# A six-layer attention stack on one core: scores, mask and maxima by halves of the heads, with a transposition between the halves

## The reference

```
def local_attention(q, k, v):          # w = 32, nw = 16 windows of a sequence
    bq = q.reshape(b, h, nw, w, d)
    bk = k.reshape(b, h, nw, w, d)
    ...                                # keys: the window before and the own one, 64 in all
    # sim = 8 * (q . k), masked to the 33 last keys, softmax over the 64 keys, times v
for each of 6 layers, each sequence:
    q, k, v = shift_tokens(x) @ Wqkv;  q, k = l2norm(.) * scale, rotary
    x = x + local_attention(q, k, v) @ Wo
    x = x + feed-forward(layernorm(shift_tokens(x)))
```

## Time and profile before

| what | value |
|---|---|
| median of 3 runs | 1909.38 us (1898.79, 1909.38, 1910.66) |
| the profiled execution's own time | 1898.89 us |
| its span, first to last instruction | 1897.1 us |
| PE busy | 1606.4 us, 85% |
| DVE busy | 1250.9 us, 66% |
| ACT busy | 989.3 us, 52% |
| the stack, first to last scores | 572.0 to 1414.8 us |
| granted TensorE clock | mean 0.927; 0.99 from 700 to 1200 us |

### The profile page before, as it was taken

How to read it: one execution, slowest core, us unless ns; L and a number is a source line. 1 busy time by engine, 2 the same in 40 slices (tenths; PEclk the granted TensorE clock), 3 DMA queues, 4 the chain that set the end, 5 groups by cost and what they waited for, 6 DMA issues and landing times.

```text
span 1897.1 us, 42488 instructions
## 1 busy us (share of the span) xinstructions
PE 1606.4 (85%) x17121; PEld 1091.3 (58%) x17121; DVE 1250.9 (66%) x2351; ACT 989.3 (52%) x1861; POOL 762.1 (40%) x1082
## 2 busy tenths in 40 slices
PE   3005476999878999999999999999987999999999
PEld 1002264676645666656666666666664677677676
DVE  6846694212957878878878778888864666666211
ACT  1034133333335667756767566666654776677332
POOL 0000030100357676776776667766740333334000
PEclk6556797899978999999999999999999999999999
DMA  3000002010032323322323232332230000000111
GB/s 111 19 6 0 3 1 63 22 35 15 1 108 52 92 74 81 84 71 70 93 73 80 76 77 64 92 83 60 57 87 1 1 1 1 1 1 1 34 34 34
DMA packets 74572, 88.23 MB, mean 47 GB/s; under 512 B 22994, under 2 KB 42936, under 8 KB 74346
## 3 DMA queue, kind: packets, MB, share of 16 engines
q1 hardware_dynamic: 73562, 85.28, 17.3%
q10 hardware_dynamic: 816, 0.24, 0.1%
HBM read 35.21 MB, written 2.34 MB: 20 GB/s over the span
## 4 chain that ended last, share of the span: by engine, by line
PE 60%; DVE 27%; issue 6%; ACT 4%; DVEq 1%; DMA 1%; POOL 0%; ACTq 0%; POOLq 0%; SPq 0%
PE PS L1412 8%; PE PS L1132 6%; PE PS L1123 6%; PE PS L1664 4%; PE PS L2162 4%; DVE st_t L1456 3%; PE PS L2119 3%; PE PS L1542 3%; PE PS L2141 3%; DVE st_r L1448 3%; DVE st_ss L1461 3%; DVE st_den L1581 2%; PE PS L1779 2%; PE PS L1616 2%; PE PS L1521 2%
## 5 line engine op out<-in xcount | busy, mean ns | idle before, releaser
L1490 POOL TENSOR_TENSOR st_r<-st_r,st_t 128x512 f32<-128x512 f32 x192 | 243.8, 1276 | 193.0 <-DVE st_t L1456 193.0
L1412 PE MATMUL PS<-st_wqkv,st_xs 128*128 128x512 f32 x576 | 306.1, 616 | 14.3 <-DVE st_t L1456 8.8
L2266 POOL TENSOR_SCALAR la_p<-la_p,la_rden 128x589 f32<-128x589 f32 x64 | 112.9, 1764 | 229.8 <-DVE la_rden L2285 229.8
L1448 DVE TENSOR_TENSOR st_r<-PS,st_rot 128x512 f32<-128x512 f32 x192 | 129.2, 673 | 102.7 <-ACT st_sqh L1432 101.9
L1507 POOL TENSOR_TENSOR st_r<-st_r,st_gy 128x512 f32<-128x512 f32 x192 | 195.1, 1049 | 3.8
L1191 ACT ACTIVATE m_h<-PS 128x512 f32<-128x512 f32 x128 | 76.1, 598 | 139.9 <-PE PS L1123 139.9
L2279 DVE TENSOR_REDUCE la_nmx<-PS 128x1 f32<-128x589 f32 x128 | 92.7, 766 | 84.8 <-PE PS L2124 84.8
L1432 ACT ACTIVATE st_sqh<-PS 128x512 f32<-128x512 f32 x192 | 114.6, 597 | 54.9 <-PE PS L1412 53.8
L2231 ACT ACTIVATE la_p<-PS,la_nmx 128x589 f32<-128x589 f32 x128 | 95.1, 748 | 82.0 <-DVE la_nmx L2279 81.9
L1216 DVE SCALAR_TENSOR_TENSOR m_y<-PS,m_g,m_y 128x128 f32<-128x128 f32 x112 | 31.5, 344 | 159.6 <-PE PS L1132 159.6
L806 POOL MEMSET l_s<- 128x144 f32 x2 | 0.4, 222 | 329.2 <-DVE x L648 215.9
(11 more groups left out here) (311 smaller groups left out, 3490.0 us busy)
## 6 DMA issues: line engine op xcount, KB each, us to landing
st_vv<-st_v SPq DMA_DIRECT2D x744, 64.0 KB, 2.0
st_wqkv<-in_st_wqkv SPq DMA_DIRECT2D x18, 512.0 KB, 4.2
m_w<-in_m_w SPq DMA_DIRECT2D x32, 256.0 KB, 3.1
st_wo<-in_st_wo SPq DMA_DIRECT2D x6, 512.0 KB
st_w<-in_st_w SPq DMA_DIRECT2D x6, 341.0 KB
la_wc<-in_la_wc SPq DMA_DIRECT2D x1, 1344.0 KB, 6.9
ca_blocks<-in_blank SPq DMA_DIRECT2D x1, 1280.0 KB, 7.0
st_qks<-in_st_qks SPq DMA_DIRECT2D x6, 128.0 KB, 4.4
```

The source lines that it names most:

```text
L1412: pe.matmul(PS[:, 2 + m % 2, :], self.xs[:, b, P * t:P * t + P], self.wqkv[:, l % 2, k, 512 * half:512 * half + 512], start=True, stop=Tru ...
L1448: dve.tensor_tensor(h3(self.r[:, t % 2, c, :]), h3(ps), self.rot[:, k, 0, t, :].unsqueeze(1) .broadcast_to([P, 8, D2]), ALU.mult)
L1490: pool.tensor_tensor(r, r, self.t2[:, c % 2, :], ALU.add).then_inc(self.added, 1)
```

## The change

The mask, the scores and the maxima are each done in two halves, e = 0 and then e = 1, one PSUM bank each. The semaphores `masked`, `scores` and `mx_ready` count halves now. TensorE waits for the first bank's mask only, does 32 matmuls in the array's upper 64 rows, then the second transposition of the outputs of T-1, and then the 32 matmuls of the lower rows. Projection 0 of a fresh turn stands behind all of that.

```
-        def pe_scores(self, pe, T):
+        def pe_scores(self, pe, T, e):
             t = T % self.TILES
-            pe.wait_ge(self.r_evac, 4 * T + 4)
-            pe.wait_ge(self.masked, T + 2)
+            if e == 0:
+                pe.wait_ge(self.r_evac, 4 * T + 4)
+            pe.wait_ge(self.masked, 2 * T + 2 + e)
             for c in range(8):
                 for w in range(4):
-                    for e in range(2):
-                        k = P * t + WIN * w
-                        mm = pe.matmul(PS[WIN * w:WIN * w + WIN, e, D2 * c:D2 * c + D2],
...
+                    k = P * t + WIN * w
+                    mm = pe.matmul(PS[WIN * w:WIN * w + WIN, e, D2 * c:D2 * c + D2],
...
-            act.activation(PS[:, 0:2, :].rearrange("p e (c k) -> p (e c) k", c=8),
-                           self.wmask[:, min(t, 1), :].unsqueeze(1).broadcast_to([P, 16, 2 * WIN]), ACT.Copy)\
-               .then_inc(self.masked, 1)
+            for e in range(2):
+                act.activation(PS[:, e, :].rearrange("p (c k) -> p c k", c=8),
+                               self.wmask[:, min(t, 1), :].unsqueeze(1).broadcast_to([P, 8, 2 * WIN]), ACT.Copy)\
+                   .then_inc(self.masked, 1)
...
-            dve.wait_ge(self.scores, T + 1)
             ps = PS[:, 0:2, :].rearrange("p e (c k) -> p e c k", c=8)
-            dve.tensor_reduce(heads(self.mx[:, :]), ps, X, ALU.max).then_inc(self.mx_ready, 1)
-            dve.wait_ge(self.mx_ready, T + 1)
+            for e in range(2):
+                dve.wait_ge(self.scores, 2 * T + 1 + e)
+                dve.tensor_reduce(self.mx[:, 8 * e:8 * e + 8], ps[:, e, :, :], X, ALU.max).then_inc(self.mx_ready, 1)
+            dve.wait_ge(self.mx_ready, 2 * T + 2)
...
                 if here:
-                    self.pe_scores(pe, T)
+                    self.pe_scores(pe, T, 0)
+                if past:
+                    self.pe_turn_o(pe, T - 1, 1)
+                if here:
+                    self.pe_scores(pe, T, 1)
                 if fresh:
                     self.pe_proj(pe, T + 2, 0)
-                if past:
-                    self.pe_turn_o(pe, T - 1, 1)
```

More of the change, by code:

```diff
@@ L1530, in act_turn_r @@
             act.activation(dst, src, ACT.Copy).then_inc(self.r_evac, 1)
-        def pe_scores(self, pe, T):
+        def pe_scores(self, pe, T, e):
             t = T % self.TILES
-            pe.wait_ge(self.r_evac, 4 * T + 4)
-            pe.wait_ge(self.masked, T + 2)
+            if e == 0:
+                pe.wait_ge(self.r_evac, 4 * T + 4)
+            pe.wait_ge(self.masked, 2 * T + 2 + e)
             for c in range(8):
                 for w in range(4):
-                    for e in range(2):
-                        k = P * t + WIN * w
-                        mm = pe.matmul(PS[WIN * w:WIN * w + WIN, e, D2 * c:D2 * c + D2],
[L1543 to L1546, removed]
+                    k = P * t + WIN * w
+                    mm = pe.matmul(PS[WIN * w:WIN * w + WIN, e, D2 * c:D2 * c + D2],
+                                   self.qT[64 * e:64 * e + 64, c, WIN * w:WIN * w + WIN],
+                                   self.kT[64 * e:64 * e + 64, c, k:k + 2 * WIN],
+                                   start=False, stop=(c == 7), skip_group_check=True,
+                                   tile_position=(64 * e, WIN * w))
             mm.then_inc(self.scores, 1)
```

## The result

The changed kernel takes 1921.49 us (median of 10 runs, 1914.99 to 1929.68) against 1907.14 for the kernel before (10 runs, 1898.79 to 1914.90): ratio 1.0079, 95% interval 1.0052 to 1.0105, +14 us between the medians. Forecast was 1926, +17, in a range of 1903 to 1944.

A forecast was written before the change was run, and what follows sets the result against it. TensorE's path from the scores to projection 2 was taken to bound turns with t = 2, 3, 0: 9 x 0.72 + 18 x 0.63 = 17.8, +0.45, -1 for code, about +17 us, median 1909.4 to 1926, range 1903 to 1944.

The forecast's parts named there:

- the bound and the sign in turns with t = 2 and 3: Scores to projection 2: TensorE sets the chain, its losses paid in full; +0.72 us fresh, +0.63 at t = 3.
- the term for t = 0: Turns with t = 0, given the same TensorE list and the same cost as t = 3: +0.63 us.
- the array: Scores' matmuls in four small tiles instead of eight: both halves 1.68 us against 1.39, +0.29 us a tile.
- Rival A: Scores: a half takes as long as the whole did; +45 us, 1954, chance 0.08.
- rival B: Scores: the number of matmuls sets the time, a half 0.70 us, switches alone cost; +7, 1916; chance 0.13 with no change.
- entries and exits: TensorE's changes between small-tile scores and other matmuls: +0.28 us in turns with t = 3, 0, 1; +0.24 fresh.
- the maxima: VectorE: two reductions of 512 take what one of 1024 does within 0.05 us, without a wait at t = 3.
- gains nothing: Output projection: gets its second operand earlier but already started right behind projection 1, so no gain.
- worth nothing on the chain, either way: Mask by halves: removes TensorE's 0.40 us wait at t = 1, where 0.93 us of slack covers it anyway.
- code loading: TensorE's nine stops in or behind the scores are code not yet there; six on the chain shrink 0.2 us each, -1.
- the +4 us: TensorE's stops: if they are not code loading, the six stopped turns pay too, some +4 us.
- Rival C: Scores: the slower burst lets code loading catch up and the waits go; -5 us, 1904, chance 0.09.

The follow-up runs named there:

- e8: Kernel before with the scores' two row groups one after the other and the mask by halves, one maximum, transposition behind both: ratio 0.9965 to before.
- e1: Kernel before with only the scores' matmuls reordered, all 32 of the first row group, then all 32 of the second: ratio 1.0053 to before.
- e3: Kernel before with the second transposition between two pieces of the scores, cut by channels so each uses both row groups; mask and maximum whole: ratio 1.0043.
- e9: Kernel before with the scores' row groups one after the other and maxima by halves, one whole mask, transposition behind both: ratio 1.0079 to before.
- e4: Changed kernel with ScalarE, in fresh turns, copying the second half of the transposed outputs ahead of projection 0's values: ratio 1.0060 to before.
- e10: e8 with one line changed: TensorE waits for both mask halves ahead of the first half of the scores: ratio 1.0051 to before.
- e5: Kernel before with 64 more waits on a semaphore long reached ahead of the stack's loop, moving the code by 32 instructions: ratio 0.9974.
- e12: Kernel before, unchanged, run again for a second profile: ratio 1.0019, profile span 1912.4 us.

## Why the prediction was right, and by what errors

**Right: the bound and the sign in turns with t = 2 and 3.** TensorE's piece between the scores and projection 2 sets the cycle there, and what it loses is paid. Cycle 3 to 0 grew by 0.56 where +0.63 was forecast.

**Too high: the term for t = 0.** "I give it the same +0.63" is not what came: cycle 0 to 1 changed by -0.04 and 1 to 2 by +0.50, together +0.46. The early mask only moves the border between the two by 0.4 us (e8). And the array's loss alone, +0.31 a burst, cost 0.04 in the two cycles together (e1).

**Right: the array.** +0.31 a burst (e1) for +0.29, from the row of `pe_mix`. Rival A, the factor of two, and rival B, no cost in the array, both fall. The Trainium skill's "up to 2x" (page "TensorEngine Tiling (Array Packing)", section "Theoretical Speedup") is 1.92 / 1.61 = 1.2x here.

**Slightly high: entries and exits**, 0.19 us a turn in e3 for 0.28. In the changed kernel the projection behind the second half takes 0.96 us to the next start, where the sum had 1.05.

**Right: the maxima.** Two reductions take 1.28 us for 1.22 and nobody waits for them in turns with t = 3; by themselves they bring nothing (e9).

**Wrong: the output projection "gains nothing".** In the fresh turn it lost. The step moved projection 0 past the transposition on TensorE's list but did not follow it to ScalarE's list, where the copy stands behind projection 0's values. Forecast for that cycle +0.72, measured +1.21; with the copy ahead, 16.43, +0.62 (e4).

**Wrong: the early mask is "worth nothing on the chain, either way".** In steady turns so it is. With the order of e1 it is worth 17 us, none of them in the steady cycles (e8 against e10 and e1). What it is worth in the changed kernel itself was not measured: no run has the move and a whole mask. The parts do not add up either: order (1.0053) and move (1.0043) less the mask's gain (0.9%) would give some 1.001, and 1.0079 was measured.

**Half right: code loading.** The stops are code, and e5 shows it, so the +4 us set against the case that they are something else falls away. The forecast had them a little shorter, -0.2 us each; they shrank from 17.7 us in nine (22.4 in the second profile) to 9.2. Rival C, *Faster*, is right in that about half of them went, and wrong in the rest: the burst did not stay cheap.

**The number.** The steady part grew by 26 us in the profiles (47 medians: 827.6 to 853.8). The forecast's 17.8 counts 27 turns; at its prices all 36 would be 12 x 0.72 + 24 x 0.63 = 24, so the steady part is near it, with the copy's wait (some 7 us) missing and t = 0 too dear. The disturbed part gave 5 us back against the first profile of before and 14 against the second, where leaving out nine turns and -1 for the stops allowed some 7. So +14 for +17 has some luck in it. The range's upper end, 1944, is the forecast with 27 x 0.7 us on top, a burst 0.7 over the forecast's and not "at +0.7".

## What to carry to other kernels

When an instruction is moved on one engine, follow what its result feeds on every other engine's list: an in-order queue that expected the old order turns a harmless move into a wait. Splitting work to start earlier is worth something only where someone waits; here the half meant for an in-order, busy VectorE brought nothing, while the half that released TensorE helped, not in the steady turns but in those that stop for code. So look at what an engine's queue may fetch once a semaphore is up, and not only at when the engine starts. And where a kernel's runs scatter by 1%, read steady cycles and disturbed turns apart before explaining a median: here they moved in opposite directions.

## What the runs showed of the hardware

- Small tiles of one row group, 64 rows by 32 columns, 64 matmuls: 1.10 us; the same count over both row groups 0.86 us.
- Code comes in blocks of 16 KB (2.24 MB in 137 packets). Where 256 matmuls and weight loads run in 1.4 us, TensorE stops up to 2.9 us for the next block (T = 17 of e12). A turn that stops does so behind the same matmul in every profile with the same code, and 32 more instructions ahead move that place by 16 matmuls (e5).
- The block begins to load 1.0 to 1.6 us behind the end of the mask whose semaphore stands ahead of the burst, in 60 of 69 stops, with that mask up 0.1 to 1.9 us ahead of the burst. A mask 0.5 us earlier makes the load start some 0.6 us earlier (T = 3, 4 and 15, e10 to e8).
- A stop of 2.5 us can be followed by some 6 us at the lower clock (T = 29 of e12: granted clock 0.50, 1.2 GHz).
